# Another order on TensorE and VectorE in the attention stage, and VectorE in place of GpSimd for the low halves of the new rows

## The reference

```python
x = x + xattn(ctx, layernorm(x))       # xattn: below, "adj_raw" is layernorm(x)
x = x + moe(layernorm(x))

def xattn(h, adj_raw):                 # Wq.T @ Wk folded: the heads are summed
    sim = einsum('bhnd,bhmd->bnm', Q, K) / (sqrt(d) * H)
    threshold = top_k(sim, int(0.3 * 512))[0][..., -1:]
    A = sigmoid(sim) * (sim >= threshold)
    A = (A + swapaxes(A, -1, -2)) * 0.5
    return (1 - gamma) * adj_raw + gamma * A

def moe(x):                            # 2048 tokens, 32 experts in 8 groups, 8 chosen for each token
    scores = sigmoid(x @ router_w)
    # top 4 groups by the sum of their best two, then top 8 experts in them
    routed = sum over the 8 of weight * ((silu(x @ gate_e) * (x @ up_e)) @ down_e)
    shared = (silu(x @ sw_gate) * (x @ sw_up)) @ sw_down
    return routed + shared
```

## Time and profile before

| what | us |
|---|---|
| median of 3 runs | 1104.59 (1103.67 to 1105.88) |
| the profiled execution, time | 1106.17 |
| its span | 1104.4 |
| attention stage, about | 322 |
| short stage, until the experts' first tile | 37.6 |
| expert stage | 744.8 |
| TensorE busy over the span | 921.8 |
| VectorE busy over the span | 573.0 |

### The profile page before, as it was taken

How to read it: one execution, slowest core, us unless ns; L and a number is a source line. 1 busy time by engine, 2 the same in 40 slices (tenths; PEclk the granted TensorE clock), 3 DMA queues, 4 the chain that set the end, 5 groups by cost and what they waited for, 6 DMA issues and landing times.

```text
span 1104.4 us, 21250 instructions
## 1 busy us (share of the span) xinstructions
PE 921.8 (83%) x4604; PEld 490.0 (44%) x4605; DVE 573.0 (52%) x1288; ACT 487.4 (44%) x993; POOL 481.6 (44%) x380
## 2 busy tenths in 40 slices
PE   3367676675787799999999999999999999999985
PEld 1143242342544455554545555545544454545542
DVE  5947686675785444445544444454454545454321
ACT  5284453462213344445444444454454545454331
POOL 2021051051343245555455456555456453655543
PEclk8568887886888899999999999999999999999998
DMA  5111021010123867677977777777878788786654
GB/s 178 59 39 50 1 77 50 30 51 1 73 70 116 255 147 162 141 171 165 259 178 159 170 174 170 166 170 173 211 157 196 211 183 237 159 183 112 122 107 71
DMA packets 90267, 149.25 MB, mean 135 GB/s; under 512 B 9648, under 2 KB 46768, under 8 KB 90224
## 3 DMA queue, kind: packets, MB, share of 16 engines
q0 software_dynamic: 33120, 80.64, 37.3%
q1 hardware_dynamic: 57104, 68.13, 18.7%
HBM read 101.55 MB, written 47.20 MB: 135 GB/s over the span
## 4 chain that ended last, share of the span: by engine, by line
PE 45%; issue 8%; DVE 4%; ACT 4%; DVEq 3%; DMA 3%; ACTq 2%; SPq 1%; POOL 0%; POOLq 0%
PE bank L256 37%; PE bank L1488 4%; DMA stage_dn<-in_L_ffn_w_down_dram 3%; PE bank L1479 3%; ACT gu L238 3%; DVEq L1159 2%; ACTq L1159 2%; DVE gu L245 1%; DVE hid L1395 1%; DVE dn L248 1%; DVE mark_p L393 1%; DVE hT L1404 0%; ACT silu L1255 0%; ACTq L238 0%; PE bank L1459 0%
## 5 line engine op out<-in xcount | busy, mean ns | idle before, releaser
L256 PE MATMUL bank<-gu,xgT 128*128 x1764 | 407.8, 381 | 12.2 <-issue 8.2
L1205 POOL DMA_INDIRECT out_dram<-y,ids_i x145 | 240.9, 1661 | 287.3 <-DMA out_dram<-y,ids_i 158.0
L256 PEld LDWEIGHTS bank<-gu,xgT 128*128 128x128 f16 x1764 | 172.9, 98 | 193.5 <-issue 22.6
L256 PE MATMUL bank<-dn,hT 128*128 x870 | 212.1, 380 | 16.7 <-issue 16.6
L1193 POOL DMA_INDIRECT xg<-xrows,ids_i x153 | 157.6, 1030 | 64.0 <-issue 41.1
L1395 DVE SCALAR_TENSOR_TENSOR hid<-bank,xg,silu 128x256 f32<-128x256 f32 x146 | 70.4, 482 | 207.7 <-ACT silu L1255 207.7
L1267 ACT CAST hT<-bank 128x256 f16<-128x256 f32 x146 | 53.7, 368 | 225.7 <-PE bank L1479 225.7
L1274 ACT ACTIVATE y<-bank 128x512 f32<-128x512 f32 x145 | 86.6, 597 | 134.4 <-PE bank L256 134.4
L1404 DVE TENSOR_TENSOR hT<-bank,hT 128x256 f16<-128x256 f32 x146 | 61.8, 423 | 151.3 <-ACT hT L1267 151.3
L256 PEld LDWEIGHTS bank<-dn,hT 128*128 128x128 f16 x870 | 84.9, 98 | 91.9 <-issue 24.8
L256 PE MATMUL bank<-xT,gu 128*128 128x512 f16 x384 | 97.3, 417 | 16.0 <-DVE hid L307 16.0
(11 more groups left out here) (217 smaller groups left out, 820.7 us busy)
## 6 DMA issues: line engine op xcount, KB each, us to landing
stage_gu<-in_L_ffn_w_gate_dram SPq DMA_DIRECT2D x32, 512.0 KB
stage_gu<-in_L_ffn_w_up_dram SPq DMA_DIRECT2D x32, 512.0 KB
stage_dn<-in_L_ffn_w_down_dram SPq DMA_DIRECT2D x32, 512.0 KB
x_sb<-in_x_dram SPq DMA_DIRECT2D x4, 1024.0 KB, 6.5
xrows<-adj SPq DMA_DIRECT2D x4, 1024.0 KB, 4.2
out_dram<-acc SPq DMA_DIRECT2D x4, 1024.0 KB, 5.4
xg<-xrows,ids_i POOLq DMA_INDIRECT x153, 4.4
out_dram<-y,ids_i POOLq DMA_INDIRECT x145, 5.1
```

The costliest lines, as they stand in the source:

```text
L256: last = nc.tensor.matmul(out_ap, stationary(a, c), moving(w, c), start=(c == 0 and (a, w) == parts[0]), stop=(c == chunks - 1 and (a, w) ...
L1205: g_.indirect_dma_start(out, bass.IndirectOffsetOnAxis(ap=ids_i[:, t:t + 1], axis=0), y[:, t % YS, :], None, compute_op=ALU.add).then_inc( ...
```

## The change

It reorders all of the attention stage's loop. On TensorE, `adjacency_T` goes ahead of all `s_down`, three `s_down` stand together behind `similarities`, `logits` goes ahead of the last `s_down`, and `sum_marks(p-1)` moves into the next iteration between pieces 2 and 3 of `s_gate_up`, with its result in another bank (`MARKB`), `copy_found`, `turn_found` and `copy_table` moving with it. On VectorE, `s_product(b,0)` moves ahead of the last search step, the other products one place forward, the `s_add` one place back each (`s_add(p,3)` behind `routing`), the marks are spread over the second half of the iteration, and search step 1 no longer stands behind them. GpSimd loses two jobs: the low halves of the rows, which VectorE now forms in `low_rows`, and `part_parts`, which becomes a compare of two tensors on VectorE. The column counts (`count_columns`) move from the head of the short stage to the end of the attention stage.

```diff
+        MARKB = (SIMB[1],) * (B - 1) + (TB[0],)
...
-            pe.wait_ge(S["xhi_ready"], RT * min(b + 2, B))
+            if b + 2 < B:
+                pe.wait_ge(S["sim_copied"], RT * (b + 3))
+            else:
+                pe.wait_ge(S["adjT_used"], RT * B)
+                pe.wait_ge(S["xhi_ready"], RT * B)
...
-        def part_parts(pool, b, g):
-            if b:
-                pool.wait_ge(S["marks_summed"], b)
-            nc.gpsimd.tensor_tensor(mark_q[:, g, :, :], upto[:, 0:2 * E].unsqueeze(1).to_broadcast([P, TOP_EXPERTS, 2 * E]),
-                                    part_of[:, g, :].unsqueeze(2).to_broadcast([P, TOP_EXPERTS, 2 * E]), ALU.subtract).then_inc(S["parts_apart"], 1)
-
         def mark_parts(dve, b, g):
             n = RT * b + g
-            dve.wait_ge(S["parts_apart"], n + 1)
-            nc.vector.tensor_scalar(mark_q[:, g, :, :], mark_q[:, g, :, :], 0.0, row_idf[:, n:n + 1], ALU.is_equal, ALU.mult).then_inc(S["marks_q_ready"], 1)
+            if b:
+                dve.wait_ge(S["marks_summed"], b)
+            nc.vector.tensor_tensor(mark_q[:, g, :, :], upto[:, 0:2 * E].unsqueeze(1).to_broadcast([P, TOP_EXPERTS, 2 * E]),
+                                    part_of[:, g, :].unsqueeze(2).to_broadcast([P, TOP_EXPERTS, 2 * E]), ALU.is_equal).then_inc(S["parts_found"], 1)
+            dve.wait_ge(S["parts_found"], n + 1)
+            nc.vector.tensor_scalar(mark_q[:, g, :, :], mark_q[:, g, :, :], row_idf[:, n:n + 1], None, ALU.mult).then_inc(S["marks_q_ready"], 1)
+
+        def mark(dve, b, g):
+            mark_slots(dve, b, g)
+            mark_parts(dve, b, g)
...
-                    for i in range(RT):
-
-                        pool.wait_ge(S["xhi_ready"], RT * b + i + 1)
-                        nc.gpsimd.tensor_tensor(xT16[:, 1, :, columns(b, i)], xT32[:, i, :, :], xT16[:, 0, :, columns(b, i)],
-                                                ALU.subtract).then_inc(S["xlo_ready"], 1)
-                    if b >= 1:
-                        pool.wait_ge(S["keys_ready"], b)
-                        for g in range(RT):
-                            part_parts(pool, b - 1, g)
...
                     if p >= 0:
                         s_gate_up(pe, p, 2)
                     if p >= 1:
-                        turn_found(pe, p - 1)
+                        sum_marks(pe, p - 1)
                     if b + 1 < B:
                         context_T(b + 1)
                     if p >= 0:
                         s_gate_up(pe, p, 3)
+                    if p >= 1:
+                        turn_found(pe, p - 1)
                     if b + 1 < B:
                         mixed(b + 1)
@@ -665,29 +674,26 @@
                     if p >= 1:
                         pe.wait_ge(S["tab_ready"], p)
                     nc.tensor.matmul(bank[MISC][0:1, FEW], ones[:, 0:1], few[:, :], start=True, stop=True).then_inc(S["few_summed"], 1)
-                    if p >= 0:
-                        s_down(pe, p, 0)
                     adjacency_T(b)
                     if p >= 0:
                         rank_tokens(pe, p)
                     if b + 1 < B:
                         similarities(b + 1)
                     if p >= 0:
-                        s_down(pe, p, 1)
-                        s_down(pe, p, 2)
+                        for i in range(RT - 1):
+                            s_down(pe, p, i)
                     rows_T(b)
+                    logits(b)
                     if p >= 0:
-                        s_down(pe, p, 3)
-                    logits(b)
+                        s_down(pe, p, RT - 1)
                     s_gate_up(pe, b, 0)
                     if b + 1 < B:
                         s_gate_up(pe, b, 1)
-                        if p >= 0:
-                            sum_marks(pe, p)
                     else:
                         sum_marks(pe, p)
                         s_gate_up(pe, b, 1, (0,))
                         rank_tokens(pe, b)
+                        count_columns()
                         s_gate_up(pe, b, 1, (1,))
                         turn_found(pe, p)
...
-                        copy_table(act, p - 1)
+                        copy_found(act, p - 1)
                     if more:
                         context_mixed(b + 1)
                     if p >= 0:
                         s_high(act, p, 2)
                         s_silu(act, p, 3)
+                    if p >= 1:
+                        copy_table(act, p - 1)
                     if more:
...
                     if p >= 0:
-                        s_product(dve, p, 0)
+                        s_product(dve, p, 1)
                         dve.wait_ge(S["xlo_ready"], RT * b)
                         dve.wait_ge(S["scores_ready"], b)
                     ch.settle()
                     for i in range(RT):
                         ch.done(v.scalar_tensor_tensor(under[:, i, :], junk[:, i, :], LOWEST, sim[:, i, :], ALU.mult, ALU.add))
+                    ch.settle()
+                    for i in range(RT):
+                        ch.done(v.max(top8[:, i, :], under[:, i, :]))
                     if p >= 0:
-                        s_product(dve, p, 1)
-                    ch.settle()
-                    for i in range(RT):
-                        ch.done(v.max(top8[:, i, :], under[:, i, :]))
+                        s_product(dve, p, 2)
                     ch.step(v.tensor_scalar(rank[:, :], cnt[:, :], -1.0, float(KEEP), ALU.mult, ALU.add))
                     ch.step(v.tensor_tensor(at_rank[:, :, :], one_to_8[:, :].unsqueeze(1).to_broadcast([P, RT, 8]),
                                             rank[:, :].unsqueeze(2).to_broadcast([P, RT, 8]), ALU.is_equal))
                     v.tensor_reduce(few[:, :], at_rank[:, :, :], AX.X, ALU.add).then_inc(S["few_ready"], 1)
                     ch.step(v.tensor_tensor(top8[:, :, :], top8[:, :, :], at_rank[:, :, :], ALU.mult))
                     ch.step(v.tensor_reduce(lo[:, :], top8[:, :, :], AX.X, ALU.add))
-                    if p >= 0:
-                        s_product(dve, p, 2)
                     if b + 1 < B:
                         x_stats(b + 1, range(0, RT // 2))
...
+                def low_rows(b):
+                    for i in range(RT):
+                        dve.wait_ge(S["xhi_ready"], RT * b + i + 1)
+                        v.tensor_tensor(xT16[:, 1, :, columns(b, i)], xT32[:, i, :, :], xT16[:, 0, :, columns(b, i)],
+                                        ALU.subtract).then_inc(S["xlo_ready"], 1)
...
                     if p >= 0:
-                        s_add(dve, p, 2)
+                        s_add(dve, p, 1)
                         find_keys(dve, ch, p)
-                        s_add(dve, p, 3)
-                        for g in range(RT):
-                            mark_slots(dve, p, g)
-                        if not more:
-                            for g in range(RT):
-                                mark_parts(dve, p, g)
+                    low_rows(b)
                     if more:
                         search_step(b + 1, 1)
+                    if p >= 0:
+                        s_add(dve, p, 2)
+                        for g in range(2 if more else RT):
+                            mark(dve, p, g)
                     routing(b)
+                    if p >= 0:
+                        s_add(dve, p, 3)
                     if more:
                         search_step(b + 1, 3)
                         if p >= 0:
-                            for g in range(RT):
-                                mark_parts(dve, p, g)
+                            mark(dve, p, 2)
                         else:
                             convert_low(dve, 1)
+                        if b == 0:
+                            dve.wait_ge(S["rows_stored"], 16)
+                            dve.wait_ge(S["zeroed"], 16)
+                        s_product(dve, b, 0)
+                        if p >= 0:
+                            mark(dve, p, 3)
                         search_step(b + 1, 4)
...
-                mark_slots(dve, b, 0)
-                mark_slots(dve, b, 1)
+                count_tiles()
+                mark(dve, b, 0)
+                mark(dve, b, 1)
                 s_product(dve, b, 1)
-                for g in range(2):
-                    mark_parts(dve, b, g)
-                for g in range(2, RT):
-                    mark_slots(dve, b, g)
-                    mark_parts(dve, b, g)
-                count_tiles()
+                mark(dve, b, 2)
+                mark(dve, b, 3)
                 s_product(dve, b, 2)
```

More of the change, by code:

```diff
@@ L180, in xattn_moe_kernel @@
         GB, UB = (5, 7), (6, 1)
+        IDS, INFO = 2, 3
         DB = (7, 5, 6, 7)
@@ L347, in turn_found @@
                 pe.wait_ge(S["scores_ready"], b + 2)
+                pe.wait_ge(S["ranks_used"], b + 1)
             for j in range(2):
@@ L357, in copy_found @@
             nc.scalar.copy(found[:, :, :].rearrange("p j (g e) -> p g e j", g=RT),
```

(24 more changed lines are left out.)

17 lines of the change are left out of this document (3 added, 14 removed).

## The result

| what | before | after |
|---|---|---|
| median, us (runs) | 1105.24 (4; 1103.67 to 1106.62) | 1066.68 (4; 1064.11 to 1068.30) |
| span of the profiled execution | 1104.4 | 1064.8 |

What follows compares the result with a forecast made beforehand. The attention loop was taken as bound by waits, with no engine saturated. Savings of 14.3 (b=1), 11.5 (b=2), 5 (b=3) and 0.3 us (short stage) made -31, hence 1074 us; forecast range 1066 to 1080.

Steps and rivals of the forecast that it cites:

- three waits of its first part: Attention loop: TensorE for `s_product(p,0)`, 4.84 us; VectorE for transposes, 6.21; after `xn`, scores 3.18, counts 2.17, marks 6.02.
- the second: VectorE's 6.21 us wait before `tmp` for the transposes, which stand behind `s_down(p,0)`.
- the new stall: Batch 3: ranks stand behind half of `s_gate_up(3,1)`, which waits for `s_add(2,3)`; the last `find_keys` idles 5 us.
- T: The moment when `bound(b)` starts its count on VectorE; offsets within a batch are from it.
- rival C: Slower: the store ahead of the x load delays x, eating the 31 us; halfway, no change; chance 0.04 for slower.
- D: VectorE's marks: the compare runs at twice the rate, giving 1071 us; chance 0.08.
- A: VectorE costs more: compare 1.21 us, full `find_keys` contention, low clock in b=1; 1085 us; 0.26 shared with B.
- B: TensorE's hold at `s_add(p,3)`: all four groups cold, few sum at T+21, not 16; 1084 us; 0.26 shared with A.
- (a): Batch front: `s_gate_up(p,1)` waits for `s_add(p,3)`, some 7 us idle, then 8.15 us; `few` sum T+16.0 instead of T+18.5.
- the situation of my text: TensorE idles some 7 us before `s_gate_up(p,1)`, which then runs at low clock; `few` sum at T+16.0.

Runs made afterwards that it cites:

- the filler run: Changed kernel with `logits` behind the last `s_down`, plus 16 unread matmuls between pieces 0 and 1 of `s_gate_up` in batches 1 and 2: 1068.3 us.
- the filler alone: Changed kernel with 12 unread matmuls on TensorE ahead of `adjacency_T` in batches 1 to 3: 1064.9 us, ratio 0.9643.
- the run with the earlier add and the filler: Changed kernel with `s_add(p,3)` in the middle of routing and 12 unread matmuls ahead of `adjacency_T`: 1059.1 us, ratio 0.9584.

## Why the prediction was right, and where its sizes were off

**The structure held.** All three waits of its first part are gone in the batches (0.8 us of the second is left), and the new stall came where it was put. `tmp` is reached at T+18.1 in b=1 (93.56 to 111.62), no scores are waited for, the last `find_keys` idles 4.91 us (5 forecast). In batches 1 to 3 VectorE waits nowhere for `x_loaded`, so rival C fell. The compare takes 0.69 us (0.65 taken), so D fell, and with it A, whose 1.21 it isn't (nor did `find_keys` take 6.2, or batch 1 run cold). B fell too: in the loop not one `s_gate_up` group between `s_add(p,3)` and the sum is cold. The chain that B prices at 21.6 us holds three such groups, not four; three cold ones in place of one would add 5.6 us (an estimate from 8.15 and 5.34), near the 5 that it reckoned with.

**The number is at the edge.** The measured 1066.7 lies 0.7 us inside the forecast's 1066 to 1080, and one of the four runs is below it: that it lies inside is partly luck. Of the 39.6 us of span 1.8 are in the expert stage, where nothing changed (see Open). The attention and the short stage gave 37.9 us, where 31 were forecast; every stretch but the first beat its forecast, so no errors cancelled.

**The step that was mis-sized is in (a)**: "TensorE idles before it: an estimate [...] some 7 us. I take the low-clock price, 8.15". It idled 1.34 us in front of the groups of batch 2 and 0.90 in front of those of batch 3 and kept 2.4 GHz. So the `few` sum ended at T+13.1, not T+16.0, and `tmp` at T+22.3, not 25.1: of the size of all that by which b=2 beat its forecast (2.7 us). In b=3 it is 1.6 of 3.1, with the sum at T+12.6 and not 14.3. The end of `s_add(p,3)` was right (22.0 us after `xn` against 22.5). The other end was wrong: `s_gate_up(b,0)`, the prediction's `s_gate_up(p,0)`, ends 20.8 us after `xn`, not 16. The copies took 4.9 us, not 6; `logits` was priced at 2 us and `s_down(p,3)` at 2.7, and they took 6.87 and 4.11 at the low clock. The 2 us for `logits` was too low at either clock: the old trace has 3.65 at the full one, with `s_down(p,3)` in front, and the reorder takes just that away. TensorE of the kernel before, batch 2 (timeline):

```profile
226.47 3.65 PE L642 MATMUL bank<-rw,under 128*128 128x32 f32 x32
```

With `logits` late the situation of my text appears on the chip (5.00 us of idling, sum at T+15.5), and the filler run shows that the loss comes back when the clock does.

**Smaller sizes.** `find_keys` in the loop took 4.0 us (4.8 forecast; 3.2 without GpSimd), since only its L382 and L386 meet GpSimd's base. Cold similarities and the wait for the squares cost +1.3, not +0.5 (`xn` ends at T+36.8: 14.4 after `tmp`, 13.1 before). From `xn` to the next T 27.3 passed, 28.1 forecast. The second half of `s_gate_up(3,1)` took 2.76 at full clock, and I had 4.0. The marks (2.12), the low rows (2.50) and routing fit. In b=1 the full clock was taken rightly: 5.34 us after 2.07 of waiting.

**GpSimd and VectorE.** Beside GpSimd's subtraction the low rows took 5.91 us, without it 2.50, and in `find_keys` one instruction of 0.18 took 1.07 beside GpSimd's rows. The Trainium skill, "GPSIMD Engine Reference", section "Key points", names two SBUF inputs or a two-port mode as the condition; the low rows (two inputs in SBUF) agree. That `part_parts` left GpSimd is worth 8 us here, and the low rows' move next to nothing by itself. The Trainium skill, "VectorE: DVE Perf Modes", section "The perf-mode tier table", gives 16-bit `tensor_tensor` twice the rate. The table says nothing of broadcast operands, and the compares here, of 512 elements at 0.69 us and of 1024 at 1.22, both with both operands broadcast, don't have that rate; no run here has a 16-bit `tensor_tensor` without a broadcast to try it on.

**Parts and whole.** Undone one by one, the transposes are worth 17 us, the product 15, `part_parts` 8 and the early `logits` 6, together 46 against the 38.6 measured, and `s_add(p,3)` behind routing costs 5.6. They all act on one loop, and each also through the clock of what stands behind; that this is why they don't add is argued, not shown.

**Open.** The expert stage is 1.8 us shorter with TensorE as busy as before (687.54 us, 687.42 in the earlier trace rows). Its code is the same in all fourteen kernels, and their traces have it at 742.6 to 748.7 us, so 1.8 us lies inside that spread and can't be put down to the change. No run undoes the third move by itself: that the marks behind search step 1 and `sum_marks` in the next iteration removed the waits for scores, counts and marks is read from the traces, and what they are worth alone isn't known; nor is it for `count_columns`. Whether low rows on GpSimd lose a little, and whether the filler alone gains, lies inside the intervals.

## What to carry to other kernels

Price the work in front of a hold at the clock that the new order gives it: the hold's length is a difference of two chains, and a chain of small matmuls can double. A product or an add that frees a buffer belongs ahead of work for which nobody waits; two of them, 0.6 us of VectorE each, were worth 15 and 5.6 us. Before you remove a bad neighbour, see whether it warmed the clock for the next: in batch 1 the transposes' move took away a wait of 6.0 us and gave 4.0.

## What the runs showed of the hardware

- Slow work at the right place helped: 32 matmuls of 128x32 took 6.87 us at 1.2 GHz and 3.65 at 2.4, and the whole kernel was 6 us quicker with the 6.87, since it closed the idle time ahead of the next group. From 134 to 143 the changed kernel's TensorE was busy 9.00 of 9 us at a granted 0.50.
- Behind 0.90, 1.34 and 2.07 us of waiting, `s_gate_up` ran at full clock; behind 3.69, 5.00 and 6.27 us it started at half (12.21 and 12.94 for 48, 7.83 for 24). Waits of 2.83 and 2.84 us, in the run with the product back, gave 7.03 for 24 each: the granted clock was 1.00 in the first microsecond and then fell to 0.50. The length of the wait isn't all: in batch 3 of the run with the earlier add and the filler, 12 matmuls behind 1.97 us took 4.40 (2.75 at full clock), with the granted clock at 0.98 in the first microsecond and 0.50 in the next 3.4. What sets the moment isn't shown here.
- Sharing with GpSimd hits tiny instructions hardest: an instruction of 128x32 on VectorE took 1.07 us beside GpSimd's low rows instead of 0.18, six times as long, while a low row on VectorE beside GpSimd's subtraction went from 0.63 us to 1.48 (2.50 and 5.91 for four).
- A 16-bit compare of two tensors, both broadcast, costs 1.22 us for 1024 elements and 0.69 for 512, and the one of 512 costs 1.64 in the short stage where GpSimd works beside it.
